# Self-attention with fp16 high and low parts: the low-part score matmul contracts 64 rows, for two row tiles side by side in the upper and lower half of the array

## The chip, the cores and the metric

One core of one Trainium2 chip. The metric is the device time of one execution, in microseconds (us); runs of the kernel before took 2059.68 to 2060.11 us, with a median of 2059.92 us.

## What is computed

The input `x` has four images of 256 channels by 64 x 64 points (4096 points each), in f32. Per image:

```python
xf   = group_norm(x, 32 groups)              # 256 x 4096
f, g = Wq @ xf, Wk @ xf                      # 64 x 4096 each
h    = Wv @ xf                               # 256 x 4096
scores = f.T @ g                             # 4096 x 4096, contraction over 64
beta = softmax(scores, axis=rows)            # over n, for each column m
out  = x + gamma * (h @ beta) + xf
```

## The kernel before

**Precision.** Every f32 operand of a matmul is split into an fp16 high part and an fp16 low part (the rest). A product is then a sum of fp16 matmuls that accumulate in one PSUM bank. For the scores the contraction has only 64 rows, so the 128 rows of the array hold both parts: `F1` has the high part of f in rows 0 to 63 and its low part in rows 64 to 127, `G1` has the high part of g in both halves, `GL` the low part of g in both halves. One matmul `F1.T @ G1` gives high f times high g plus low f times high g, a second one `F1.T @ GL` adds high f times low g and low f times low g.

**Tiling.** The 4096 columns of an image are cut into 16 blocks of 256 (`M`), which makes 64 steps `k` over the four images. The 4096 rows n of the scores are cut into 32 tiles of 128, in 8 groups `g` of 4 tiles. One score group is a PSUM tile `S` of 128 x 1024 f32 (two banks, each with two tiles of 256 columns); `scores(q)` (L299 to L309) issues its 8 matmuls, 2 for each tile (L307, L308). Before it TensorE waits until ScalarE has copied the group before out of `S` (`s_stored`). The copy lands in `SC` (L423); VectorE folds it into the running column maxima (L551 to L558) and later subtracts the maxima (L571); ScalarE takes the exponential twice, once to fp16 (L429, `PH`) and once to f32 (L430); GpSimd makes the low part of the weights (L240, `PL`).

**Order.** The loop over `n` (512 iterations, `n = 8k + g`) is software-pipelined by hand. In iteration n TensorE issues the scores of step k + 2 (`scores(n + 2 * G)`, L382), the transposes that turn the maxima and the outputs (L330, L340, L348), at times a part of the next image's projections, and then `weigh(n)` (L311 to L324), which multiplies the weights of group g with the values: 24 matmuls, 3 for each of 4 tiles and 2 column halves. Steps 62 and 63 have no scores left to issue.

**Projections.** `project_fg(u)` (L275 to L285) makes f and g of 512 points (unit u, 8 per image) with 6 matmuls of 512 columns; the weights `wqkh`, `wqkl` hold Wq in columns 0 to 63 and Wk in 64 to 127, so f comes out in PSUM rows 0 to 63 and g in rows 64 to 127. ScalarE rounds them with three casts (`round_fg`, L432 to L437) and VectorE makes the low parts with three subtractions (`low_fg`, L574 to L579), the last of which raises `fg_done`. For the first image this runs in a prologue (L354 to L361) together with the first 8 score groups; the next 8 score groups run with the value projections (L362 to L371). For the later images the units run inside the loop: `FG_AT` (L48) puts units 0 to 4 in step 13 of an image at g = 3 to 7, and units 5 to 7 in step 14 at g = 3 to 5. The scores of the next image's first block are issued in step 14 and wait for `fg_done` (L381): group g there waits for unit g. `project_v(u)` (L287) makes the values of 4 row tiles with 24 matmuls.

**VectorE's extra work.** In steps 1 to 4 of an image VectorE also measures the next image (L678), in step 5 it makes its variances (L682), in step 6 its inverse roots (L684), in steps 7 to 10 it normalises it (L688).

**Inputs.** SyncE's queue loads the first image, then the weights and gamma (L178 to L183); ScalarE's first cast of the weights waits for all of them (`w_in`, L445).

Of the kernel before, what the change touches and what calls it, by code (L numbers as in the profile page):

```python
# [5 lines left out]
def groupnorm_attention(nc, x, wqT, wkT, wvT, gamma, out):  # L6
    f32, f16, i32 = mybir.dt.float32, mybir.dt.float16, mybir.dt.int32
    ALU, ACT, AX = mybir.AluOpType, mybir.ActivationFunctionType, mybir.AxisListType

    BATCH, C, N = x.shape  # L10
    P = 128
    H = C // P
    CQ = wqT.shape[1]
    M = 256
# [3 lines left out]
    GT = 4  # L18
# [5 lines left out]
    NFG = N // FGW  # L24
# [30 lines left out]
    with ExitStack() as ctx:  # L55
        def sb(name, shape, dt):
            return ctx.enter_context(nc.sbuf_tensor(name, shape, dt))

        def sem(name):
            return ctx.enter_context(nc.semaphore(name))  # L60

        F1 = sb("F1", [P, N], f16)
        G1 = sb("G1", [P, N], f16)
        GL = sb("GL", [P, N], f16)
        V = sb("V", [P, T * VW], f16)
        XH = sb("XH", [P, H, N], f16)
        XL = sb("XL", [P, H, N], f16)

        wqk = sb("wqk", [P, H, P], f32)
        wv = sb("wv", [P, H, C], f32)  # L70
        wqkh = sb("wqkh", [P, H, P], f16)
        wqkl = sb("wqkl", [P, H, P], f16)
        wvh = sb("wvh", [P, H, C], f16)
        wvl = sb("wvl", [P, H, C], f16)
        gam = sb("gam", [P, 1], f32)
# [32 lines left out]
        S = ctx.enter_context(nc.psum_tensor("S", [P, GW], f32))  # L108
# [3 lines left out]
        w_in = sem("w_in")  # L112
# [16 lines left out]
        fg_hi = sem("fg_hi")  # L129
        fg_done = sem("fg_done")  # L130
# [21 lines left out]
        def sc(s):  # L152
# [2 lines left out]
            first = (k % 2) * T * M + g * GW  # L155
            return SC[:, first:first + GW]

        def piece(p):
            return slice(p * PC, (p + 1) * PC)

# [15 lines left out]
        @block.sync  # L176
        def _(sp):
            for q in range(NPC):  # L178
                sp.dma_start(x0[:, :, piece(q)], xv[0, :, :, piece(q)]).then_inc(x0_in[q], 16)
            sp.dma_start(wqk[:, :, 0:CQ], wqT.rearrange("(h p) q -> p h q", p=P)).then_inc(w_in, 16)  # L180
            sp.dma_start(wqk[:, :, CQ:P], wkT.rearrange("(h p) q -> p h q", p=P)).then_inc(w_in, 16)
            sp.dma_start(wv[:, :, :], wvT.rearrange("(h p) v -> p h v", p=P)).then_inc(w_in, 16)
            sp.dma_start(gam[:, :], gamma).then_inc(w_in, 16)  # L183

            def residual_input(k):
                b, j = divmod(k, CPB)
                sp.dma_start(xres[:, :, :], xv[b, :, :, j * M:(j + 1) * M]).then_inc(xres_in, 16)

            def store(k):
                b, j = divmod(k, CPB)  # L190
                sp.wait_ge(out_ready, k + 1)
                sp.dma_start(ov[b, :, :, j * M:(j + 1) * M], RES[:, k % 2, :, :]).then_inc(out_stored[k % 2], 16)

            def load(b, p):
                sp.dma_start(xin[:, :, :], xv[b, :, :, piece(p)]).then_inc(xin_in, 16)

            residual_input(0)
            for k in range(K):
                b, j = divmod(k, CPB)
                if k > 0:  # L200
                    store(k - 1)
                if k + 1 < K:
                    sp.wait_ge(res_ready, k + 1)
                    residual_input(k + 1)
                if b + 1 < BATCH:
                    p = j - STAT_FIRST + 1
                    if 0 <= p < NPC:
                        if p > 0:
                            sp.wait_ge(xin_read, b * NPC + p)
                        elif b > 0:  # L210
                            sp.wait_ge(xl_ready[1], NPC * (b + 1))
                            sp.wait_ge(xl_ready[0], NPC * (b + 1))
                        load(b + 1, p)
                    p = j - NORM_FIRST + 1
                    if j == STAT_FIRST + NPC - 1:
                        sp.wait_ge(xin_read, (b + 1) * NPC)
                        load(b + 1, 0)
                    elif 0 < p < NPC:
                        sp.wait_ge(xl_ready[1], NPC * (b + 1) + p)
                        load(b + 1, p)  # L220
            store(K - 1)
            for parity in range(2):
                sp.wait_ge(out_stored[parity], 16 * K // 2)
# [48 lines left out]
        def _(pe):  # L272
            mm = nc.tensor.matmul

            def project_fg(u, o):  # L275

                b, i = divmod(u, NFG)
                for h in range(H):
                    pe.wait_ge(xl_ready[h], b * NPC + i // 2 + 1)
                n = slice(i * FGW, (i + 1) * FGW)  # L280
                for h in range(H):
                    mm(o, wqkh[:, h, :], XH[:, h, n], start=h == 0, stop=False)  # L282
                    mm(o, wqkl[:, h, :], XH[:, h, n], start=False, stop=False)  # L283
                    m = mm(o, wqkh[:, h, :], XL[:, h, n], start=False, stop=h == H - 1)  # L284
                m.then_inc(fg_ready, 1)  # L285

            def project_v(u, pair):  # L287
                g = u % G
                for i in range(GT):
                    t = g * GT + i  # L290
                    o = O[:, pair, i // 2, (i % 2) * C:(i % 2 + 1) * C]
                    for h in range(H):
                        xh, xl = XH[:, h, t * P:(t + 1) * P], XL[:, h, t * P:(t + 1) * P]
                        mm(o, xh, wvh[:, h, :], start=h == 0, stop=False)  # L294
                        mm(o, xh, wvl[:, h, :], start=False, stop=False)  # L295
                        m = mm(o, xl, wvh[:, h, :], start=False, stop=h == H - 1)  # L296
                m.then_inc(v_ready, 1)

            def scores(q):  # L299

                k, g = divmod(q, G)
                cols = slice((k % CPB) * M, (k % CPB + 1) * M)
                if q > 0:
                    pe.wait_ge(s_stored, q)
                for i in range(GT):
                    f = F1[:, (g * GT + i) * P:(g * GT + i + 1) * P]
                    mm(S[:, i * M:(i + 1) * M], f, G1[:, cols], start=True, stop=False)  # L307
                    m = mm(S[:, i * M:(i + 1) * M], f, GL[:, cols], start=False, stop=True)  # L308
                m.then_inc(s_ready, 1)  # L309

            def weigh(n):  # L311
# [42 lines left out]
            for i in range(NFG + 3):  # L354
                if i < NFG:
                    if i >= 4:
                        pe.wait_ge(fg_done, i - 3)
                    project_fg(i, O[:, i // 2 % 2, i % 2, :])
                if i >= 3:
                    pe.wait_ge(fg_done, i - 2)  # L360
                    scores(i - 3)  # L361
            for g in range(G):  # L362
                scores(G + g)
# [9 lines left out]
            for n in range(K * G):  # L373
                k, g = divmod(n, G)
# [3 lines left out]
                if k + 2 < K:  # L378
                    nb, i = divmod(k + 2, CPB)
                    if i == 0:  # L380
                        pe.wait_ge(fg_done, nb * NFG + g + 1)  # L381
                    scores(n + 2 * G)  # L382
                if g == 2:
                    if k > 0:
# [5 lines left out]
                u = next_fg(k, g)  # L390
# [5 lines left out]
                u = late_values(k, g)  # L396
# [21 lines left out]
        def _(act):  # L418
# [13 lines left out]
            def round_fg(u, o):  # L432
                n = slice(u % NFG * FGW, (u % NFG + 1) * FGW)
                act.wait_ge(fg_ready, u + 1)
                nc.scalar.copy(F1[0:CQ, n], o[0:CQ, :])
                nc.scalar.copy(G1[CQ:P, n], o[CQ:P, :])
                nc.scalar.copy(G1[0:CQ, n], o[CQ:P, :]).then_inc(fg_hi, 1)  # L437

            def round_v(u, pair):
                first = u % G * GT * VW  # L440
# [1 line left out]
                act.wait_ge(v_ready, u + 1)  # L442
                nc.scalar.copy(vh, O[:, pair, :, :].rearrange("p m (t c) -> p (m t) c", c=C)).then_inc(v_hi, 1)  # L443

            act.wait_ge(w_in, 64)  # L445
            nc.scalar.copy(wqkh[:, :, :], wqk[:, :, :])
            nc.scalar.copy(wvh[:, :, :], wv[:, :, :]).then_inc(w_hi, 1)
            for q in range(NPC):
# [17 lines left out]
            for n in range(K * G):  # L466
                k, g = divmod(n, G)
# [3 lines left out]
                u = next_fg(k, g)  # L471
                if u is not None:
                    round_fg(u, O[:, (k + 1) % 2, u % 2, :])
                u = late_values(k, g)
# [4 lines left out]
                if g == 6 and b + 1 < BATCH and NORM_FIRST <= j < NORM_FIRST + NPC:  # L479
                    p = j - NORM_FIRST  # L480
# [5 lines left out]
        def _(dve):  # L486
            ve = nc.vector
# [86 lines left out]
            def low_fg(u, o):  # L574
                n = slice(u % NFG * FGW, (u % NFG + 1) * FGW)
                dve.wait_ge(fg_hi, u + 1)
                ve.tensor_tensor(F1[CQ:P, n], o[0:CQ, :], F1[0:CQ, n], ALU.subtract)
                ve.tensor_tensor(GL[0:CQ, n], o[CQ:P, :], G1[CQ:P, n], ALU.subtract)
                ve.tensor_tensor(GL[CQ:P, n], o[CQ:P, :], G1[CQ:P, n], ALU.subtract).then_inc(fg_done, 1)  # L579

            def low_v(u, pair):
                first = u % G * GT * VW
# [64 lines left out]
            for n in range(K * G):  # L647
                k, g = divmod(n, G)
                b, j = divmod(k, CPB)
                q = n + 2 * G - 1  # L650
# [15 lines left out]
                u = next_fg(k, g)  # L666
                if u is not None:
                    low_fg(u, O[:, (k + 1) % 2, u % 2, :])
                u = late_values(k, g)
                if u is not None:  # L670
                    low_v(u, (k + 1) % 2)
                if g == 5 and b + 1 < BATCH:
                    if STAT_FIRST <= j < STAT_FIRST + NPC:
                        p = j - STAT_FIRST
# [10 lines left out]
                    if NORM_FIRST <= j < NORM_FIRST + NPC:  # L685
                        p = j - NORM_FIRST
# [30 lines left out]
```

## Time and profile before

| | |
|---|---|
| Median of 3 runs | 2059.92 us (2059.68 to 2060.11) |
| Profiled execution, its own time | 2059.63 us |
| Its span, first to last instruction | 2057.8 us |
| Mean granted TensorE clock | 0.997 |
| TensorE matmul busy | 98% of the span |
| VectorE, ScalarE, GpSimd busy | 79%, 78%, 60% |
| Matmuls recorded | 17984 |

The busy share of an engine is the part of the span in which it had an instruction under way. A matmul's duration in the trace is modelled and overlaps that of the next one; the pace of TensorE is read from start to start.

### The profile page before, as it was taken

What the parts mean: (1) busy time and instruction counts of PE and PEld (TensorE: products, weight loads), DVE (VectorE), ACT (ScalarE), POOL (GpSimd) and SP (SyncE); (2) the same over time, 40 slices, a digit from 0 to 9 for tenths busy, and PEclk for the clock granted to TensorE, in tenths of its full rate; (3) what the DMA queues carried; (4) which work ended last, traced back from release to release, by engine and by line L of the source; (5) the groups of instructions that cost most, each with busy time, mean ns of one, the idle gap of its engine ahead of it and who ended that gap; (6) DMA issues with size and microseconds to landing.
All of it is one profiled execution on the core that took longest, in us unless ns stands there. A gap on an engine that the chain in (4) does not pass through costs nothing.

```text
span 2057.8 us, 42838 instructions
## 1 busy us (share of the span) xinstructions
PE 2006.9 (98%) x17984; PEld 1758.9 (85%) x17984; DVE 1620.9 (79%) x2208; ACT 1612.0 (78%) x1699; POOL 1236.6 (60%) x675
## 2 busy tenths in 40 slices
PE   3899999999999999999999999999999999999999
PEld 1688888888888888888888888888878888888887
DVE  8787898877868889887876878988787677777774
ACT  4587788888867777887877778888787787777875
POOL 2066667775545666876544666677645466666666
PEclk9999999999999999999999999999999999999999
DMA  2011101100001110110000111011000000000000
GB/s 94 1 42 53 62 17 42 58 22 16 17 11 57 62 42 16 63 37 22 17 17 32 48 51 37 23 61 37 22 14 14 16 17 22 22 17 22 16 22 21
DMA packets 43585, 66.05 MB, mean 32 GB/s; under 512 B 3201, under 2 KB 36225, under 8 KB 43393
## 3 DMA queue, kind: packets, MB, share of 16 engines
q1 hardware_dynamic: 43392, 63.32, 9.1%
q8 instruction: 141, 2.31, 0.5%
q14 instruction: 52, 0.42, 0.1%
HBM read 46.53 MB, written 16.78 MB: 31 GB/s over the span
## 4 chain that ended last, share of the span: by engine, by line
PE 95%; DVE 2%; ACT 1%; DMA 1%; issue 1%; SPq 0%; ACTq 0%; DVEq 0%
PE O L322 22%; PE O L323 22%; PE O L321 22%; PE S L307 11%; PE S L308 11%; PE O L348 1%; PE O L294 1%; PE O L330 1%; PE O L296 1%; PE O L295 1%; PE MB L340 1%; DMA SC<-x 1%; PE O L284 1%; PE O L283 1%; PE O L282 1%
## 5 line engine op out<-in xcount | busy, mean ns | idle before, releaser
L240 POOL TENSOR_TENSOR PL<-SC,PH 128x1024 f16<-128x1024 f32 x512 | 1092.6, 2135 | 783.2 <-ACT SC L430 782.9
L322 PE MATMUL O<-V,PH 128*128 128x256 f16 x4096 | 1119.7, 273 | 0.0
L321 PE MATMUL O<-V,PH 128*128 128x257 f16 x4096 | 1115.8, 272 | 2.0 <-DVE GL L579 2.0
L323 PE MATMUL O<-V,PL 128*128 128x257 f16 x4096 | 1113.0, 272 | 0.0
L423 ACT ACTIVATE SC<-S 128x1024 f32<-128x1024 f32 x512 | 524.5, 1024 | 337.4 <-PE S L308 334.8
L558 DVE TENSOR_TENSOR XM<-SC,XM 128x512 f32<-128x512 f32 x896 | 619.9, 692 | 156.9 <-ACT SC L423 136.7
L571 DVE TENSOR_TENSOR SC<-SC,MB 128x1024 f32<-128x1024 f32 x512 | 621.0, 1214 | 57.5 <-PE MB L340 56.8
L429 ACT ACTIVATE PH<-SC 128x1024 f16<-128x1024 f32 x512 | 537.6, 1050 | 9.9 <-PE O L323 9.1
L430 ACT ACTIVATE SC<-SC 128x1024 f32<-128x1024 f32 x512 | 536.5, 1048 | 0.0
L307 PE MATMUL S<-G,F 128*128 128x256 f16 x2048 | 477.8, 274 | 11.7 <-ACT SC L423 6.2
L308 PE MATMUL S<-GL,F 128*128 128x256 f16 x2048 | 477.9, 274 | 0.0
L323 PEld LDWEIGHTS O<-V,PL 128*128 128x128 f16 x4096 | 402.5, 98 | 52.1
L321 PEld LDWEIGHTS O<-V,PH 128*128 128x128 f16 x4096 | 394.1, 96 | 60.2 <-issue 2.8
L322 PEld LDWEIGHTS O<-V,PH 128*128 128x128 f16 x4096 | 396.2, 97 | 56.0
L307 PEld LDWEIGHTS S<-G,F 128*128 128x128 f16 x2048 | 201.0, 98 | 39.0 <-DVE GL L579 8.9
L308 PEld LDWEIGHTS S<-GL,F 128*128 128x128 f16 x2048 | 201.0, 98 | 24.0
L585 DVE TENSOR_TENSOR V<-O,V 128x1024 f16<-128x1024 f32 x32 | 39.2, 1225 | 79.9 <-ACT V L443 79.9
L249 POOL TENSOR_SCALAR RES<-xres,rscale,rbias 128x256 f32<-128x256 f32 x128 | 82.3, 652 | 0.0
L564 DVE TENSOR_REDUCE mxc<-O 128x2 f32<-128x512 f32 x64 | 44.2, 691 | 45.8 <-PE O L330 45.8
L443 ACT CAST V<-O 128x1024 f16<-128x1024 f32 x32 | 32.4, 1013 | 53.0 <-PE O L296 53.0
L294 PE MATMUL O<-wvh,XH 128*128 128x256 f16 x256 | 70.3, 275 | 3.4 <-DVE mxc L564 2.2
L295 PE MATMUL O<-wvl,XH 128*128 128x256 f16 x256 | 70.2, 274 | 0.0
(73 smaller groups left out, 980.3 us busy)
## 6 DMA issues: line engine op xcount, KB each, us to landing
xin<-x SPq DMA_DIRECT2D x24, 1024.0 KB, 5.4
xres<-x SPq DMA_DIRECT2D x64, 256.0 KB, 2.7
out<-RES SPq DMA_DIRECT2D x64, 256.0 KB, 2.1
SC<-x SPq DMA_DIRECT2D x4, 1024.0 KB, 8.3
wv<-wvT SPq DMA_DIRECT2D x1, 256.0 KB, 10.2
wqk<-wqT SPq DMA_DIRECT2D x1, 64.0 KB, 10.4
wqk<-wkT SPq DMA_DIRECT2D x1, 64.0 KB, 10.3
gam<-gamma SPq DMA_DIRECT2D x1, 0.5 KB, 9.7
```

The costliest lines, as they stand in the source:

```text
L240: pool.tensor_tensor(PL[:, s % RING, :], sc(s), PH[:, s % RING, :], ALU.subtract).then_inc(pl_ready, 1)
L294: mm(o, xh, wvh[:, h, :], start=h == 0, stop=False)
L307: mm(S[:, i * M:(i + 1) * M], f, G1[:, cols], start=True, stop=False)
L308: m = mm(S[:, i * M:(i + 1) * M], f, GL[:, cols], start=False, stop=True)
L321: mm(o[:, 0:C + 1], PH[:, n % RING, cols], vh, start=t == 0, stop=False)
L322: mm(o[:, 0:C], PH[:, n % RING, cols], vl, start=False, stop=False)
L323: w = mm(o[:, 0:C + 1], PL[:, n % RING, cols], vh, start=False, stop=t == T - 1)
L423: nc.scalar.activation(sc(q), S[:, :], ACT.Copy).then_inc(s_stored, 1)
L429: nc.scalar.activation(PH[:, s % RING, :], sc(s), ACT.Exp, bias=SHIFT)
L430: nc.scalar.activation(sc(s), sc(s), ACT.Exp, bias=SHIFT).then_inc(exp_done, 1)
L558: ve.tensor_tensor(XM[:, :], part, XM[:, :], ALU.max).then_inc(s_maxed, 1)
L571: ve.tensor_tensor(tile, tile, MB[:, 0:M].unsqueeze(1).to_broadcast([P, GT, M]), ALU.subtract).then_inc(sub_ready, 1)
```

## The change

Three things change. First, `project_fg` of an odd unit uses weights with Wk in the first and Wq in the last 64 columns (a third copy block of Wq is loaded behind Wk), so that f and g of odd units come out with the halves exchanged; `round_fg` and `low_fg` follow (`halves`). `F1` then holds the high part of f in rows 0 to 63 for even units and in rows 64 to 127 for odd ones. Second, a score group takes two row tiles from an even unit (places 0 and 1, first bank of `S`) and two from the next, odd unit (places 2 and 3, second bank); `project_v` places the values in the same order, and the waits on `fg_done` ask for both units of a pair. Third, the second score matmul of a tile contracts only the 64 rows that hold the high part of f: the product of the two low parts is no longer computed. These four matmuls are issued between the first two and the last two full ones, in the order upper, lower, upper, lower half.

```diff
-        wqk = sb("wqk", [P, H, P], f32)
+        wqk = sb("wqk", [P, H, P + CQ], f32)
...
+        def tile(g, i):
+
+            return (g - g % 2 + i // 2) * GT + g % 2 * 2 + i % 2
+
+        def halves(u):
+
+            top, bottom = slice(0, CQ), slice(CQ, P)
+            return (bottom, top) if u % 2 else (top, bottom)
...
+            sp.dma_start(wqk[:, :, P:P + CQ], wqT.rearrange("(h p) q -> p h q", p=P)).then_inc(w_in, 16)
...
+                w = slice(i % 2 * CQ, i % 2 * CQ + P)
                 for h in range(H):
-                    mm(o, wqkh[:, h, :], XH[:, h, n], start=h == 0, stop=False)
...
+                    mm(o, wqkh[:, h, w], XH[:, h, n], start=h == 0, stop=False)
...
-                    t = g * GT + i
+                    t = tile(g, i)
...
-                for i in range(GT):
-                    f = F1[:, (g * GT + i) * P:(g * GT + i + 1) * P]
-                    mm(S[:, i * M:(i + 1) * M], f, G1[:, cols], start=True, stop=False)
-                    m = mm(S[:, i * M:(i + 1) * M], f, GL[:, cols], start=False, stop=True)
+                tiles = [slice(tile(g, i) * P, (tile(g, i) + 1) * P) for i in range(GT)]
+                for i in (0, 2):
+                    mm(S[:, i * M:(i + 1) * M], F1[:, tiles[i]], G1[:, cols], start=True, stop=False)
+                for i in (0, 2, 1, 3):
+                    half = slice(0, CQ) if i < 2 else slice(CQ, P)
+                    mm(S[:, i * M:(i + 1) * M], F1[half, tiles[i]], GL[half, cols], start=i % 2 == 1, stop=i % 2 == 0)
+                for i in (1, 3):
+                    m = mm(S[:, i * M:(i + 1) * M], F1[:, tiles[i]], G1[:, cols], start=False, stop=True)
                 m.then_inc(s_ready, 1)
...
-                    pe.wait_ge(fg_done, i - 2)
+                    pe.wait_ge(fg_done, (i - 3) // 2 * 2 + 2)
...
-                        pe.wait_ge(fg_done, nb * NFG + g + 1)
+                        pe.wait_ge(fg_done, nb * NFG + g // 2 * 2 + 2)
...
-                nc.scalar.copy(F1[0:CQ, n], o[0:CQ, :])
-                nc.scalar.copy(G1[CQ:P, n], o[CQ:P, :])
-                nc.scalar.copy(G1[0:CQ, n], o[CQ:P, :]).then_inc(fg_hi, 1)
+                f, g = halves(u)
+                nc.scalar.copy(F1[f, n], o[f, :])
+                nc.scalar.copy(G1[g, n], o[g, :])
+                nc.scalar.copy(G1[f, n], o[g, :]).then_inc(fg_hi, 1)
...
-            act.wait_ge(w_in, 64)
+            act.wait_ge(w_in, 80)
...
-                ve.tensor_tensor(F1[CQ:P, n], o[0:CQ, :], F1[0:CQ, n], ALU.subtract)
-                ve.tensor_tensor(GL[0:CQ, n], o[CQ:P, :], G1[CQ:P, n], ALU.subtract)
-                ve.tensor_tensor(GL[CQ:P, n], o[CQ:P, :], G1[CQ:P, n], ALU.subtract).then_inc(fg_done, 1)
+                f, g = halves(u)
+                ve.tensor_tensor(F1[g, n], o[f, :], F1[f, n], ALU.subtract)
+                ve.tensor_tensor(GL[f, n], o[g, :], G1[g, n], ALU.subtract)
+                ve.tensor_tensor(GL[g, n], o[g, :], G1[g, n], ALU.subtract).then_inc(fg_done, 1)
```

## Rows read from the trace of the kernel before

**Rows 1.** The page: busy time of each engine, and the chain that ended last.

```profile
PE 2006.9 (98%) x17984; PEld 1758.9 (85%) x17984; DVE 1620.9 (79%) x2208; ACT 1612.0 (78%) x1699; POOL 1236.6 (60%) x675
...
PE 95%; DVE 2%; ACT 1%; DMA 1%; issue 1%; SPq 0%; ACTq 0%; DVEq 0%
```

**Rows 2.** Busy time of the engines by stretch: us, then PE, PEld, DVE, ACT, POOL.

```profile
0.00:70.00 70.00, 30.03 (x148) 16.62 (x149) 58.93 (x103) 33.14 (x45) 13.41 (x11) 0.90 0.19 70
70.00:110.00 40.00, 35.81 (x323) 31.18 (x321) 30.15 (x36) 27.82 (x30) 10.67 (x5) 1.00 0.01 1
110.00:500.00 390.00, 390.00 (x3539) 345.52 (x3537) 321.58 (x442) 318.17 (x332) 260.72 (x140) 1.00 0.12 40
```

**Rows 3.** Groups of score matmuls and weight loads: busy us, mean ns, idle before.

```profile
L308 PE MATMUL S<-GL,F 128*128 128x256 f16 x2048 | 477.9, 274 | 0.0
L307 PE MATMUL S<-G,F 128*128 128x256 f16 x2048 | 477.8, 274 | 11.7 <-ACT SC L423 6.2 <-DVE GL L579 5.4
...
L308 PEld LDWEIGHTS S<-GL,F 128*128 128x128 f16 x2048 | 201.0, 98 | 24.0
```

**Rows 4.** TensorE in order of time, one score group: start us, us, line.

```profile
201.80 0.38 PE L340 MATMUL MB<-ident,mxc 128*128 128x128 f32 x2
...
202.02 0.27 PE L307 MATMUL S<-G,F 128*128 128x256 f16 x1
...
202.78 0.27 PE L308 MATMUL S<-GL,F 128*128 128x256 f16 x1
...
202.89 0.27 PE L321 MATMUL O<-V,PH 128*128 128x257 f16 x1
```

**Rows 5.** In order of time: TensorE after a wait, at the start of step 14.

```profile
515.72 0.69 DVE L579 TENSOR_TENSOR GL<-O,G 64x512 f16<-64x512 f32 x1
515.73 0.27 PE L308 MATMUL S<-GL,F 128*128 128x256 f16 x1
...
516.64 0.10 PEld L321 LDWEIGHTS O<-V,PH 128*128 128x128 f16 x1 [0.93 <-issue]
516.67 0.27 PE L321 MATMUL O<-V,PH 128*128 128x257 f16 x1 [0.68 <-DVE GL L579]
...
516.78 0.27 PE L322 MATMUL O<-V,PH 128*128 128x256 f16 x1
```

**Rows 6.** In order of time: units 5 and 7 of the second image, step 14.

```profile
529.18 0.38 PE L284 MATMUL O<-XL,wqkh 128*128 128x512 f16 x1
529.39 0.27 PE L321 MATMUL O<-V,PH 128*128 128x257 f16 x1
...
532.26 0.27 PE L307 MATMUL S<-G,F 128*128 128x256 f16 x1
...
532.80 0.69 DVE L579 TENSOR_TENSOR GL<-O,G 64x512 f16<-64x512 f32 x1
...
539.24 0.27 PE L321 MATMUL O<-V,PH 128*128 128x257 f16 x1
...
541.88 0.27 PE L307 MATMUL S<-G,F 128*128 128x256 f16 x1
...
542.64 0.69 DVE L579 TENSOR_TENSOR GL<-O,G 64x512 f16<-64x512 f32 x1
```

**Rows 7.** VectorE in order of time: its first subtraction of two units in succession.

```profile
509.50 0.69 DVE L577 TENSOR_TENSOR F<-O,F 64x512 f16<-64x512 f32 x1
...
514.32 0.68 DVE L577 TENSOR_TENSOR F<-O,F 64x512 f16<-64x512 f32 x1
```

**Rows 8.** Busy time by step of 29.24 us, columns as in Rows 2: steps 1, 5, 6.

```profile
137.35:166.59 29.24, 29.24 (x268) 26.00 (x267) 24.02 (x33) 23.32 (x25) 18.17 (x11) 1.00 0.17 55
...
254.31:283.55 29.24, 29.24 (x268) 25.99 (x267) 26.30 (x42) 23.32 (x25) 18.17 (x11) 1.00 0.06 19
283.55:312.79 29.24, 29.24 (x268) 26.00 (x267) 27.00 (x46) 23.44 (x25) 18.20 (x11) 1.00 0.06 19
```

**Rows 9.** ScalarE in order of time, start of the kernel.

```profile
23.52 2.00 ACT L451 CAST XH<-SC 128x1024 f16<-128x1024 f32 x2 [7.63 <-DVE SC L540]
```

More of the change, by code:

```diff
@@ L67, in groupnorm_attention @@
         XL = sb("XL", [P, H, N], f16)
-        wqk = sb("wqk", [P, H, P], f32)
+        wqk = sb("wqk", [P, H, P + CQ], f32)
         wv = sb("wv", [P, H, C], f32)
-        wqkh = sb("wqkh", [P, H, P], f16)
-        wqkl = sb("wqkl", [P, H, P], f16)
+        wqkh = sb("wqkh", [P, H, P + CQ], f16)
+        wqkl = sb("wqkl", [P, H, P + CQ], f16)
         wvh = sb("wvh", [P, H, C], f16)
@@ L280, in project_fg @@
                 n = slice(i * FGW, (i + 1) * FGW)
+                w = slice(i % 2 * CQ, i % 2 * CQ + P)
                 for h in range(H):
-                    mm(o, wqkh[:, h, :], XH[:, h, n], start=h == 0, stop=False)
-                    mm(o, wqkl[:, h, :], XH[:, h, n], start=False, stop=False)
-                    m = mm(o, wqkh[:, h, :], XL[:, h, n], start=False, stop=h == H - 1)
+                    mm(o, wqkh[:, h, w], XH[:, h, n], start=h == 0, stop=False)
+                    mm(o, wqkl[:, h, w], XH[:, h, n], start=False, stop=False)
+                    m = mm(o, wqkh[:, h, w], XL[:, h, n], start=False, stop=h == H - 1)
                 m.then_inc(fg_ready, 1)
```

## The prediction

> **What bounds the kernel now.** I read the busy times and the chain that ended last first [rows 1]. TensorE is busy for 98% of the span and makes 95% of the chain, with the other engines at 79% and below; what the change saves on TensorE counts, until another engine is in the way. By stretch [rows 2] TensorE has no idle time from 110 to 500 us (390.00 of 390.00), and the stretches behind it look alike, but for short waits around the units of the next image. Only the first 70 us belong to others: there TensorE is busy for 30.03 and VectorE for 58.93 us. From start to start, not by modelled durations, TensorE's pace is: 8 score matmuls from 202.02 to 202.89, so 0.87 us or 0.109 each [rows 4]. The weight loads are hidden: 98 ns each [rows 3], begun as the matmul ahead of them starts.
>
> The profiled execution took 2059.63 us, 0.3 under the median of the runs; the sum goes by 2059.6.
>
> **Score matmuls.** Before, a group takes 8 slots of 0.109 us. After it are 4 full matmuls and 4 of 64 rows, in two pairs that use different halves of the array and different banks of `S`. If a pair takes one slot, the group takes 6 slots: 2 x 0.109 = 0.218 us less. A pair can't take less than a slot, since a slot goes by columns: a matmul of 512 columns holds TensorE from 529.18 to 529.39, one of 257 for 0.11 [rows 6]; 64 rows still stream 256 columns. Of the 512 groups the first 8 sit in the prologue, where VectorE sets the pace, and 8 beside the first value projections, where TensorE has gaps (35.81 of 40 us) [rows 2]; I count neither. The other 496 give 496 x 0.218 = **-108.1 us**.
>
> **Stagger within a pair.** The second half starts only when its weights are in. After a wait a load stands 0.03 us before its matmul (516.64 to 516.67) [rows 5]. If the lower half's load goes only when the upper matmul has started, the pairs and the full matmul behind them end 0.03 us late in each group: 496 x 0.03 = 14.9 us. If it is pulled ahead, as a load is now, it is nothing. No row decides; I take half, **+7.4 us**, and keep 0 and 14.9.
>
> **Going over between 128 and 64 rows.** Each group changes its shape twice, into the halves and back: 992 times in 496 groups. No row has a matmul of 64 rows. The lower bound is 0: f32 transposes stand directly between fp16 matmuls, two from 201.80 and the next line at 202.02, 0.11 us each [rows 4], so one change of what the array does costs nothing. A gain is excluded, a shape change does no work. The upper bound is that the next matmul waits until the one before has left altogether and then loads: 0.273 from start to modelled end, less the slot of 0.109, is 0.164 us, with the load 0.194 [rows 3, 5]. That is 0 to 992 x 0.194 = 192 us, which is more than the whole gain. I take **0**, because the transposes are the nearest rows, but it is the weakest step. The Trainium skill speaks against it ("TensorEngine Tiling (Array Packing)", Key Properties): changing the tiling mode, not just the tile, drains TensorE. It gives no time for a drain; no row here shows one, and the rivals below carry it.
>
> **The waits on pairs of units.** In step 14 group 4 of the next image's scores now waits for unit 5 and group 6 for unit 7, each projected just one iteration earlier. Unit 5's last matmul gives way at 529.39; the scores of group 4 start at 532.26; VectorE ends the unit at 532.80 + 0.69 = 533.49 [rows 6], and a waiting matmul starts 0.26 after such an end (515.72 + 0.69 against 516.67 [rows 5]). So TensorE would stand from 532.26 to 533.75, 1.5 us. Unit 7: 542.64 + 0.69 + 0.26 = 543.59 against 541.88 [rows 6], 1.7 us. TensorE is the bound and its queue is in order, so `weigh` behind the wait is late too: 3.2 us x 3 images = **+9.6 us**. The wait of 0.68 us at the start of step 14 [rows 5] grows by the 0.22 us by which TensorE comes earlier: **+0.7 us** for three.
>
> **VectorE as the next limit.** With units 0 to 4 of step 13 an iteration takes 0.87 + 6 x 0.215 + 2.64 = 4.80 us on TensorE, and VectorE shows the same 4.82 from unit to unit, with no idle time [rows 7]. At 4.6 us on TensorE VectorE is the limit: 0.2 x 5 units x 3 = **+3 us**. An ordinary step takes 29.24 us and would take 29.24 - 8 x 0.218 = 27.5. VectorE's busy time is 24.0 in steps 1 to 4, which fits; steps 5 and 6, with variances and roots, have 26.30 and 27.00 [rows 8], nearly full. A lead of four groups covers most; I take 0.7 us an image, **+2 us**, with 0 and 6 as ends.
>
> **Edits at nothing.** The third weight transfer of 64 KB, the wider cast and the wider subtraction: ScalarE stands for 7.63 us after its weight casts [rows 9], waiting for VectorE. Without that cover it is under 1 us. The prologue's waits on pairs fall where VectorE is behind anyway. The casts and subtractions of exchanged halves, and the reordered values, have the same sizes and counts.
>
> **Sum.** 2059.6 - 108.1 + 7.4 + 0 + 9.6 + 0.7 + 3 + 2 = 1974.2, so 1974 us. Own range: 1974 - 7 - 3 - 3 = 1961 to 1974 + 7 + 4 = 1985. The Trainium skill ("TensorE: Matmul & The Clock Gate", Part 3, The mechanism) has the matmuls of different tiles starting about 4 ns apart; by that the stagger would be 2 us in place of 7.4 and the sum an estimated 1969.
>
> **Rivals.** (1) *A short drain.* The shape change costs something between the exposed load, 0.03, and just under break-even. Gain without it is 2059.6 - 1974 = 86 us, so break-even is at 86 / 992 = 0.086 us per change. At 0.03 it is 1974 + 30 = 2004, at 0.06 2033, at 0.09 2063. For it: 64 rows are another configuration, unlike a transpose over the full array. Against it: gapless rows [rows 4].
>
> (2) *A full drain, slower than before.* Each change waits for the matmul ahead to end and then loads: 0.164 to 0.194 us. The time is 1974 + 992 x 0.164 = 2137 to 1974 + 192 = 2166, less some 5 us that VectorE then no longer costs: 2132 to 2161. It decides from 0.086 us up. For it: if the array has to be empty, the modelled end is the only end that the rows know. Against: nothing in the trace waits so now. By the rule of the Trainium skill named above ("TensorEngine Tiling (Array Packing)", Key Properties) this rival or the one before it holds.
>
> (3) *The halves don't run together.* Each of the 64-row matmuls takes its own slot; then 8 slots stay, the waits on units stay, and it is 2059.6 + 9.6 = 2069, or a few us more. For it: each matmul here starts a full slot behind the one ahead, never sooner [rows 4]. Against: all those use the same rows of the array.
>
> **How the numbers follow.** Forecast 0.42, short drain 0.23, full drain 0.27, no overlap 0.08. The likeliest is 1974 us, its own range 1961 to 1985. The cases of both signs hold much, so the whole range is wide: from 1960 to 2134, with the full drain beyond its lower edge left out (about 0.17) and some 0.02 below. A difference of 0.2%, 4 us, is about what a measurement of this kernel can tell from none. Faster: 0.42 and most of the short drain, 0.62; within 0.2%: 0.03; slower: 0.27 + 0.08, 0.35.
>
> **What the profile after would show.** Right: in a score group the two starts of a pair of 64-row matmuls stand under 0.04 us apart, the first full matmul behind the halves starts 0.11 after the last pair, and the group takes about 0.67 us from its first matmul to the first of `weigh`. A short or full drain: gaps of 0.03 to 0.19 ahead of the first half and of the full matmul behind. No overlap: four starts 0.11 apart. The waits: TensorE idle some 1.5 us twice in step 14, released by the last subtraction of `low_fg`. VectorE: its idle time in step 6 gone, TensorE waiting there only if I am wrong about the lead. Steps of 27.5 us in place of 29.24 confirm the sum; steps over 29.24 refute it.

## The result, and the profile after

The changed kernel takes 2070.8 us (2068.5 to 2071.3, 5 runs) where the kernel before took 2059.9 beside it: a ratio of 1.0049, with a 95% interval of 1.0034 to 1.0063. It is slower by 11 us. The forecast was 1974 us; the number lies within the wide range, but the sign is the other one. The runs of either kernel fall in two bunches some 2 us apart, the slower one with a slightly lower mean clock (0.994 against 0.995 in the changed kernel), and bunch against bunch the loss is 9 to 10 us.

| | before | after |
|---|---|---|
| Median | 2059.92 us | 2070.81 us |
| Span of the profiled execution | 2057.8 us | 2069.4 us |
| One score group, first start to `weigh` | 0.87 us | 0.86 us |
| One ordinary step | 29.24 us | 29.19 us |
| First reduction of turned maxima in the loop (step 0) | 109.9 us | 116.2 us |

From the page of the changed kernel, the busy times and the groups of the score matmuls and of their loads (busy us, mean ns, idle before); they answer to [rows 1, 3]:

```profile
PE 2007.0 (97%) x17984; PEld 1574.7 (76%) x17984; DVE 1618.8 (78%) x2208; ACT 1613.4 (78%) x1699; POOL 1236.7 (60%) x675
...
L318 PE MATMUL S<-G,F 128*128 128x256 f16 x1024 | 196.6, 274 | 23.0 <-DVE GL L596 16.3
L321 PE MATMUL S<-GL,F 64*128 64x256 f16 x2048 | 201.6, 275 | 0.0
L323 PE MATMUL S<-G,F 128*128 128x256 f16 x1024 | 201.6, 279 | 0.0
L321 PEld LDWEIGHTS S<-GL,F 64*128 64x128 f16 x2048 | 58.3, 94 | 108.7 <-issue 108.7
L323 PEld LDWEIGHTS S<-G,F 128*128 128x128 f16 x1024 | 58.1, 97 | 108.8 <-issue 108.8
```

TensorE is as busy as before, 2007 us against 2006.9, although 2048 matmuls now run in pairs. (Busy time goes by modelled ends, 0.27 us from a start; a gap shorter than that tail doesn't show as idle.) The new thing stands at the weight loads: ahead of each stretch of halves (L321) and of each first full matmul behind it (L323) the loads sit idle for 0.21 us, 512 times each, "issue" by the profile, so no semaphore is what they wait for. Before, all of them began with the matmul ahead. The changed kernel in order of time, one score group, against [rows 4]:

```profile
204.28 0.27 PE L338 MATMUL O<-V,PL 128*128 128x257 f16 x1
204.28 0.21 PEld L318 LDWEIGHTS S<-G,F 128*128 128x128 f16 x2
204.39 0.38 PE L318 MATMUL S<-G,F 128*128 128x256 f16 x2
204.70 0.11 PEld L321 LDWEIGHTS S<-GL,F 64*128 64x128 f16 x4 [0.21 <-issue]
204.70 0.39 PE L321 MATMUL S<-GL,F 64*128 64x256 f16 x4
...
205.02 0.11 PEld L323 LDWEIGHTS S<-G,F 128*128 128x128 f16 x2 [0.21 <-issue]
205.03 0.39 PE L323 MATMUL S<-G,F 128*128 128x256 f16 x2
205.15 0.10 PEld L336 LDWEIGHTS O<-V,PH 128*128 128x128 f16 x1
205.25 0.27 PE L336 MATMUL O<-V,PH 128*128 128x257 f16 x1
```

A row of several matmuls runs from the first start to the last modelled end, so the last start is the end less 0.27 or 0.28. The four halves need 0.39 - 0.28 = 0.11 from first to last start: two pairs, one slot apart. The second full matmul starts at 204.50, its slot ends at 204.61, and the halves start at 204.70: 0.09 lost. The second pair starts at 204.81, its slot ends at 204.92, the full matmul starts at 205.03: 0.11 lost. Six slots of 0.109 and 0.206 us of gaps are 0.86 us, one hundredth less than eight slots. The gain is there, and two changes of shape eat it. (Starts are read to 0.01 us here; the whole step gives the price more sharply, see below.)

The steps say the same. The reduction of the maxima comes once a step; first the changed kernel, then the one before:

```profile
116.15 0.68 DVE L580 TENSOR_REDUCE mxc<-O 128x2 f32<-128x512 f32 x1
143.56 0.69 DVE L580 TENSOR_REDUCE mxc<-O 128x2 f32<-128x512 f32 x1 [0.90 <-PE O L345]
172.75 0.69 DVE L580 TENSOR_REDUCE mxc<-O 128x2 f32<-128x512 f32 x1 [0.91 <-PE O L345]
```

```profile
109.88 0.69 DVE L564 TENSOR_REDUCE mxc<-O 128x2 f32<-128x512 f32 x1
137.35 0.69 DVE L564 TENSOR_REDUCE mxc<-O 128x2 f32<-128x512 f32 x1 [0.91 <-PE O L330]
166.59 0.69 DVE L564 TENSOR_REDUCE mxc<-O 128x2 f32<-128x512 f32 x1 [0.91 <-PE O L330]
```

172.75 - 143.56 = 29.19 against 29.24: 0.05 us a step, 3 us in all. Two slots less in each of 8 groups should have taken 8 x 0.218 = 1.74 us off a step; 16 changes of shape took back 1.69 of it, 0.106 us each. And the changed kernel enters the loop 6.3 us late. The rest is the new waits, here TensorE in step 14 of the first image:

```profile
539.10 0.39 PE L318 MATMUL S<-G,F 128*128 128x256 f16 x2 [1.11 <-DVE GL L596]
...
550.21 0.39 PE L318 MATMUL S<-G,F 128*128 128x256 f16 x2 [1.33 <-DVE GL L596]
```

The idle time counts from the modelled end of the matmul ahead. Its slot had ended 0.16 us earlier, so the two waits cost 1.27 and 1.49, or 2.8 us an image and 8.3 in three; the second and third images show the same 1.11 and 1.33. The balance: +6.3 + 8.3 - 3 = 11.6, which is 2069.4 - 2057.8.

### The profile page after: what moved, and what is told of

It is laid out like the page before. It is cut to its first block, busy times and chain, and to the rows that moved or that the text cites. A ratio compares the mean times of both kernels' runs of the same rounds, so it can differ in the third digit from the quotient of the medians.

```text
span 2069.4 us, 42839 instructions
## 1 busy us (share of the span) xinstructions
PE 2007.0 (97%) x17984; PEld 1574.7 (76%) x17984; DVE 1618.8 (78%) x2208; ACT 1613.4 (78%) x1699; POOL 1236.7 (60%) x675
## 4 chain that ended last, share of the span: by engine, by line
PE 94%; DVE 3%; ACT 1%; issue 1%; DMA 1%; SPq 0%; ACTq 0%; DVEq 0%
PE O L337 21%; PE O L338 21%; PE O L336 21%; PE S L323 8%; PE S L321 8%; PE S L318 5%; PE O L305 1%; PE O L307 1%; PE O L306 1%; PE O L363 1%; PE O L345 1%; PE MB L355 1%; DMA SC<-x 1%; PE O L293 1%; PE O L294 1%
## 5 line engine op out<-in xcount | busy, mean ns | idle before, releaser
L318 PE MATMUL S<-G,F 128*128 128x256 f16 x1024 | 196.6, 274 | 23.0 <-DVE GL L596 16.3
L321 PE MATMUL S<-GL,F 64*128 64x256 f16 x2048 | 201.6, 275 | 0.0
L323 PE MATMUL S<-G,F 128*128 128x256 f16 x1024 | 201.6, 279 | 0.0
L321 PEld LDWEIGHTS S<-GL,F 64*128 64x128 f16 x2048 | 58.3, 94 | 108.7 <-issue 108.7
L323 PEld LDWEIGHTS S<-G,F 128*128 128x128 f16 x1024 | 58.1, 97 | 108.8 <-issue 108.8
L318 PEld LDWEIGHTS S<-G,F 128*128 128x128 f16 x1024 | 99.1, 98 | 39.8 <-DVE GL L596 20.7
```

The costliest lines, as they stand in the source:

```text
L318: mm(S[:, i * M:(i + 1) * M], F1[:, tiles[i]], G1[:, cols], start=True, stop=False)
L321: mm(S[:, i * M:(i + 1) * M], F1[half, tiles[i]], GL[half, cols], start=i % 2 == 1, stop=i % 2 == 0)
L323: m = mm(S[:, i * M:(i + 1) * M], F1[:, tiles[i]], G1[:, cols], start=False, stop=True)
```

## The experiments

**1. Two theories of the loss of 11 us.** First the changed kernel with full height in all score matmuls, then the kernel before with nothing but the waits on pairs.

```diff
-                    half = slice(0, CQ) if i < 2 else slice(CQ, P)
-                    mm(S[:, i * M:(i + 1) * M], F1[half, tiles[i]], GL[half, cols], start=i % 2 == 1, stop=i % 2 == 0)
+                    mm(S[:, i * M:(i + 1) * M], F1[:, tiles[i]], GL[:, cols], start=i % 2 == 1, stop=i % 2 == 0)
```

> The changed kernel with 128 rows in the four low-part matmuls again, everything else as changed. Theory (each change between 128 and 64 rows costs 0.103 us, 992 to 1024 times): 8 slots and no shape change, group 0.87 us, no gaps in it, steps 29.24 us; 2070.8 + 3 = 2074 us if the waits and the start-up keep their whole price, and not less than 2066. Rival (the 64-row pairs cost two slots each, no change of shape costs anything): the same 0.87 us, so this run alone does not part them, but both say that the loss of 11 us is the waits and the start-up. Rival (exchanged halves or the tile order cost time of their own on other engines): casts or subtractions longer than 0.58 and 0.69 us.

Measured: 2073.0 us (2072.3 to 2073.8). The gaps are gone, four low matmuls from 204.36 stand in slots of 0.109:

```profile
204.14 0.38 PE L318 MATMUL S<-G,F 128*128 128x256 f16 x2
204.36 0.60 PE L320 MATMUL S<-GL,F 128*128 128x256 f16 x4
204.80 0.38 PE L322 MATMUL S<-G,F 128*128 128x256 f16 x2
205.01 0.27 PE L335 MATMUL O<-V,PH 128*128 128x257 f16 x1
```

```diff
-                    pe.wait_ge(fg_done, i - 2)
+                    pe.wait_ge(fg_done, (i - 3) // 2 * 2 + 2)
...
-                        pe.wait_ge(fg_done, nb * NFG + g + 1)
+                        pe.wait_ge(fg_done, nb * NFG + g // 2 * 2 + 2)
```

> The kernel before with the two waits on pairs of units alone, nothing else changed. Theory (the whole loss is these waits): inside the loop 1.1 + 1.3 us for each of three images, 7.3 us, and what the later first score group costs in the start-up, up to 6 us: 2067 to 2074 us. Rival (the start-up loss belongs to the wider weights or to the 64-row matmuls): 2067 us and the first turn of the maxima in step 0 within 1 us of 109.9.

Measured: 2072.6 us (2072.0 to 2073.4), a ratio of 1.0060 (1.0046 to 1.0074). Two lines of waits make the whole loss, and more than it. The same two waits stand in step 14 (1.13 and 1.35 us), and the loop is entered 3.9 us later than in the kernel before:

```profile
113.79 0.68 DVE L564 TENSOR_REDUCE mxc<-O 128x2 f32<-128x512 f32 x1
```

The rival that puts the whole loss in the start-up down to the weights or the halves falls: 3.9 of the 6.3 us come without either. What the 64-row matmuls bring for themselves is the changed kernel against full height: 2073.0 - 2070.8 = 2.2 us. By that a change of shape costs (0.218 - 2.2 / 496) / 2 = 0.107 us.

**2. Is the gap a change of shape, and what does it hang on?** Two halves first, then four full ones, then two halves, in the same number of matmuls:

```diff
-                for i in (0, 2):
-                    mm(S[:, i * M:(i + 1) * M], F1[:, tiles[i]], G1[:, cols], start=True, stop=False)
-                for i in (0, 2, 1, 3):
-                    half = slice(0, CQ) if i < 2 else slice(CQ, P)
-                    mm(S[:, i * M:(i + 1) * M], F1[half, tiles[i]], GL[half, cols], start=i % 2 == 1, stop=i % 2 == 0)
-                for i in (1, 3):
-                    m = mm(S[:, i * M:(i + 1) * M], F1[:, tiles[i]], G1[:, cols], start=False, stop=True)
+                for i in (0, 2):
+                    half = slice(0, CQ) if i < 2 else slice(CQ, P)
+                    mm(S[:, i * M:(i + 1) * M], F1[half, tiles[i]], GL[half, cols], start=True, stop=False)
+                for i in (0, 2):
+                    mm(S[:, i * M:(i + 1) * M], F1[:, tiles[i]], G1[:, cols], start=False, stop=True)
+                for i in (1, 3):
+                    mm(S[:, i * M:(i + 1) * M], F1[:, tiles[i]], G1[:, cols], start=True, stop=False)
+                for i in (1, 3):
+                    half = slice(0, CQ) if i < 2 else slice(CQ, P)
+                    m = mm(S[:, i * M:(i + 1) * M], F1[half, tiles[i]], GL[half, cols], start=False, stop=True)
```

> The same matmuls in another order: two halves, four full ones, two halves, so four changes of shape in a group in place of two. The first halves follow weigh and the last are followed by weigh, which writes other banks. Theory (a change of shape costs 0.103 us wherever it stands): 2 x 0.103 more in each of 512 groups, of which some 496 count, 2070.8 + 102 = 2173 us, group 1.07 us to the first of weigh. Rival (the gap is a wait of a matmul for the one ahead that writes the same bank): no gap ahead of the first halves and behind the last ones, only the two inside, 2071 us. Rival (the gap is the first load alone, 0.03): +30, 2101 us.

Measured: 2176.2 us, 105.3 more than the changed kernel for 992 more changes: 0.106 each. In order of time, one group of it:

```profile
208.26 0.27 PE L341 MATMUL O<-V,PL 128*128 128x257 f16 x1
208.47 0.28 PE L319 MATMUL S<-GL,F 64*128 64x256 f16 x2
208.68 0.39 PE L321 MATMUL S<-G,F 128*128 128x256 f16 x2
208.91 0.38 PE L323 MATMUL S<-G,F 128*128 128x256 f16 x2
209.23 0.28 PE L326 MATMUL S<-GL,F 64*128 64x256 f16 x2
209.44 0.28 PE L339 MATMUL O<-V,PH 128*128 128x257 f16 x1
```

Every change is 0.21 from start to start where 0.109 is the slot: 208.26 to 208.47 in, 208.47 to 208.68 out, 209.02 to 209.23 in, 209.23 to 209.44 out. The first and the last join matmuls that write different banks (`O` and `S`), so the rival of the bank falls, and at 0.106 so does the one that put the gap at 0.03. A pair itself takes 0.28, as one matmul: its two halves start within 0.01 us of each other.

**3. Do the halves run together because they lie in different rows?** All four in the upper half, in the place of the choice by `i`:

```diff
-                    half = slice(0, CQ) if i < 2 else slice(CQ, P)
+                    half = slice(0, CQ)
```

> All four 64-row matmuls use the upper half of the array; for the two tiles of the odd unit they so multiply the low part of f instead of the high part. Theory (halves run together only when they lie in different rows, a pair takes one slot): four slots in place of two, 496 x 0.218 = 108 us more, 2179 us; starts 0.11 us apart. Rival (64-row matmuls are simply quick, wherever they lie): no more than 2071 us.

Measured: 2177.9 us, 107 more. The four now need 0.61 - 0.28 = 0.33 from first to last start, three slots:

```profile
206.40 0.38 PE L318 MATMUL S<-G,F 128*128 128x256 f16 x2
206.72 0.61 PE L321 MATMUL S<-GL,F 64*128 64x256 f16 x4
207.26 0.39 PE L323 MATMUL S<-G,F 128*128 128x256 f16 x2
```

**4. The price of a pair, without more changes.** Each pair issued twice:

```diff
-                for i in (0, 2, 1, 3):
+                for i, r in ((0, 0), (2, 0), (0, 1), (2, 1), (1, 0), (3, 0), (1, 1), (3, 1)):
...
-                    mm(S[:, i * M:(i + 1) * M], F1[half, tiles[i]], GL[half, cols], start=i % 2 == 1, stop=i % 2 == 0)
+                    mm(S[:, i * M:(i + 1) * M], F1[half, tiles[i]], GL[half, cols],
+                       start=i % 2 == 1 and r == 0, stop=i % 2 == 0 and r == 1)
```

> Each pair of 64-row matmuls is issued twice, so the low product is added twice; two more pairs in the same stretch, no more changes of shape. Theory (a pair costs one slot of 0.109, a change 0.103, apart from each other): 496 x 0.218 = 108 us more, 2179 us. Rival (the gap belongs to each pair): 496 x 0.42 = 208 us more, 2279 us. Rival (a stretch has a minimum time that two pairs do not fill): less than 60 us more.

Measured: 2178.8 us, 108.0 more, so a pair is 0.109 us, one slot, and the gaps are apart from it.

**5. What the forecast took the change to be:** six slots and no change of shape. From the full-height kernel, the low product of the last two tiles left out:

```diff
-                    mm(S[:, i * M:(i + 1) * M], F1[:, tiles[i]], G1[:, cols], start=True, stop=False)
-                for i in (0, 2, 1, 3):
-                    mm(S[:, i * M:(i + 1) * M], F1[:, tiles[i]], GL[:, cols], start=i % 2 == 1, stop=i % 2 == 0)
+                    mm(S[:, i * M:(i + 1) * M], F1[:, tiles[i]], G1[:, cols], start=True, stop=i == 2)
+                for i in (0, 1):
+                    mm(S[:, i * M:(i + 1) * M], F1[:, tiles[i]], GL[:, cols], start=i == 1, stop=i == 0)
                 for i in (1, 3):
-                    m = mm(S[:, i * M:(i + 1) * M], F1[:, tiles[i]], G1[:, cols], start=False, stop=True)
+                    m = mm(S[:, i * M:(i + 1) * M], F1[:, tiles[i]], G1[:, cols], start=i == 3, stop=True)
```

> The run with 128 rows in all score matmuls, and the low product left out for the last two tiles of each group: six slots in a group and no change of shape, which is what the forecast took the change to be. Theory (the shape changes are what ate the gain, the other terms stand): 2073.0 - 108.1 = 1964.9, plus the 5 us that were put down to VectorE in steps 5, 6 and 13: 1965 to 1970 us. Rival (another engine stands right behind TensorE, so that the time could not have fallen by much anyway): over 2000 us, with waits of TensorE on ScalarE, VectorE or GpSimd in every step.

Measured: 1970.7 us (1969.0 to 1971.5), a ratio of 0.9564 (0.9548 to 0.9580). Its step is 27.5 us (136.63 to 164.13 from reduction to reduction), as forecast. What the next limit costs shows in steps 6 and 7 of each image, behind VectorE's extra work; TensorE waits there for ScalarE's copy of the scores and for VectorE's subtraction of the maxima:

```profile
297.46 0.28 PE L318 MATMUL S<-G,F 128*128 128x256 f16 x1 [0.73 <-ACT SC L437]
...
309.20 0.29 PE L354 MATMUL MB<-ident,mxc 128*128 128x128 f32 x1 [0.79 <-DVE SC L586]
```

From the ends of the slots these are 0.16 us more each, 1.8 us an image. From the first reduction in the loop (115.74 and 111.34) to the last (2029.03 and 1924.23) this kernel is 100.4 us shorter than the one with full height, where 62 steps of 1.74 would be 108.1: the loop loses 7.7 us, 5.5 of them in these two waits, and the other 4.4 us of the difference between the two profiled executions come from the start-up.

**6. Half as many changes, the same slots.** On the kernel of experiment 8: even groups issue each pair twice, odd groups leave the low product out.

```diff
+                low = [(0, 0), (2, 0), (0, 1), (2, 1), (1, 0), (3, 0), (1, 1), (3, 1)] if g % 2 == 0 else []
...
-                    mm(S[:, i * M:(i + 1) * M], F1[:, tiles[i]], G1[:, cols], start=True, stop=False)
-                for i in (0, 2, 1, 3):
+                    mm(S[:, i * M:(i + 1) * M], F1[:, tiles[i]], G1[:, cols], start=True, stop=not low)
+                for i, r in low:
...
-                    mm(S[:, i * M:(i + 1) * M], F1[half, tiles[i]], GL[half, cols], start=i % 2 == 1, stop=i % 2 == 0)
+                    mm(S[:, i * M:(i + 1) * M], F1[half, tiles[i]], GL[half, cols],
+                       start=i % 2 == 1 and r == 0, stop=i % 2 == 0 and r == 1)
...
-                    m = mm(S[:, i * M:(i + 1) * M], F1[:, tiles[i]], G1[:, cols], start=False, stop=True)
+                    m = mm(S[:, i * M:(i + 1) * M], F1[:, tiles[i]], G1[:, cols], start=not low, stop=True)
```

> The kernel with the units moved forward; even groups issue each of their pairs twice, odd groups leave the low product out (their second tile pair too, so the low product is doubled in one half of the rows and missing in the other). Slots and matmuls are the same, the changes of shape are half as many. Theory (only the number of changes counts): 496 x 0.103 = 51 us less than 2060.3, 2009 us. Rival (a longer stretch costs more on the way out, or the even and odd groups cannot be averaged since other engines wait): over 2030 us.

Measured: 2015.9 us, 44.4 less than experiment 8 and 7 more than expected. An ordinary step shrinks from 29.19 to 28.35 us (139.42 to 167.77): 0.84 for 8 changes, 0.105 each, and 62 such steps would be 52 us. What is missing is 2.6 us an image in steps 5 to 10, where VectorE has its extra work. The profile shows two waits of TensorE there, 0.52 and 0.80 us, which are 0.68 and 0.96 from the ends of the slots. The rest is four starts of a score group 0.36 behind the start ahead, 0.25 late each, of which this is one:

```profile
359.03 0.27 PE L341 MATMUL O<-V,PL 128*128 128x257 f16 x1
...
359.39 0.28 PE L320 MATMUL S<-G,F 128*128 128x256 f16 x1
```

0.68 + 0.96 + 4 x 0.25 = 2.6 us, 7.9 in three images, and 52 less 7.9 is the 44 that the loop gained (1902 to 1858 us from its first reduction of the maxima to its last). So the other engines do wait, as the rival had it, but for a small part of its price, and the number of changes counts.

**7. The start-up, first try.** TensorE projects one unit further before it waits for the pair:

```diff
-                if i < NFG:
-                    if i >= 4:
-                        pe.wait_ge(fg_done, i - 3)
-                    project_fg(i, O[:, i // 2 % 2, i % 2, :])
+                for u in (3, 4) if i == 3 else (i + 1,) if i > 3 else (i,):
+                    if u < NFG:
+                        if u >= 4:
+                            pe.wait_ge(fg_done, u - 3)
+                        project_fg(u, O[:, u // 2 % 2, u % 2, :])
```

> The changed kernel; in the start-up TensorE projects unit i + 1 before it waits for the pair and issues the scores of group i - 3. Theory (the start-up loses its 6 us because TensorE stands for 6.75 us before the first scores, with unit 4 behind them): 2070.8 - 3 to 6 = 2065 to 2068 us. Rival (the start-up is paced by VectorE and what is lost is a later rise of the granted clock): within 1 us of 2070.8.

Measured: 2068.5 us (2067.9 to 2070.8), 2.3 less than the changed kernel, and the two spreads overlap. The first reduction in the loop stood at 115.79, hardly earlier. So the first wait was not what decides; neither expectation is met cleanly.

**8. The waits in step 14.** On experiment 7, the later images' units moved forward:

```diff
-    FG_AT = {(FG_FIRST, 3 + i): i for i in range(5)} | {(FG_FIRST + 1, 3 + i): 5 + i for i in range(3)}
+    FG_AT = {(FG_FIRST, 3): (0, 1), (FG_FIRST, 4): (2,), (FG_FIRST, 5): (3,), (FG_FIRST, 6): (4,),
+             (FG_FIRST, 7): (5,), (FG_FIRST + 1, 3): (6,), (FG_FIRST + 1, 4): (7,)}
...
-                    if k % CPB in (FG_FIRST + 1, FG_FIRST + 2):
-                        pe.wait_ge(fg_done, min(b + 1, BATCH - 1) * NFG + (5 if k % CPB == FG_FIRST + 1 else 8))
+                        pe.wait_ge(fg_done, min(b + 1, BATCH - 1) * NFG + (6 if k % CPB == FG_FIRST + 1 else 8))
```

> The kernel of the run before and, for the later images, the units moved forward: two in the third iteration of step 13, then one in each, so that units 6 and 7 stand in the iterations 3 and 4 of step 14. Theory (the waits of 1.1 and 1.3 us in step 14 go, the one of 0.68 at its start grows to 1 or 2): 3 x 1.5 = 4 us less than the run before, 2061 to 2064 us. If all were saved the kernel would stand at the 0.05 us a step that shape changes leave, 2057 us, level with the kernel before. Rival (VectorE, full in step 13, falls behind and hands the wait on): no gain over the run before.

Measured: 2060.3 us (2059.4 to 2062.4), 8.2 less than experiment 7, twice what I had expected. Both waits are gone (8.3 us), and the one at the start of step 14 did not grow: 2.1 us in three images, where the kernel before has 2.0.

```profile
PE O L337 <- DVE GL L596: 2.1, 3, 0.8
```

This is all that TensorE waits for the low parts behind the start-up. The ratio to the kernel before is 1.0003 (0.9994 to 1.0012).

**9. The start-up, second try.** In order of time, what TensorE waits for in the start-up; before, and changed:

```profile
58.20 0.37 PE L307 MATMUL S<-G,F 128*128 128x256 f16 x1 [1.21 <-ACT SC L423]
61.27 0.37 PE L307 MATMUL S<-G,F 128*128 128x256 f16 x1 [1.21 <-DVE GL L579]
64.25 0.40 PE L307 MATMUL S<-G,F 128*128 128x256 f16 x1 [1.11 <-ACT SC L423]
```

```profile
61.96 0.61 PE L318 MATMUL S<-G,F 128*128 128x256 f16 x2 [2.21 <-DVE GL L596]
64.85 0.59 PE L318 MATMUL S<-G,F 128*128 128x256 f16 x2 [1.21 <-ACT SC L438]
67.63 0.60 PE L318 MATMUL S<-G,F 128*128 128x256 f16 x2 [1.12 <-ACT SC L438]
```

In both, VectorE's last unit releases a group at 61 or 62 us. Before it is group 7 and one more follows; in the changed kernel it is group 6 and two follow, 2.9 us each. To let the last units pass ahead, VectorE now takes the maxima two units later:

```diff
-            for i in range(NFG + 3):
+            for i in range(NFG + 5):
...
-                if i >= 3:
-                    maximum(i - 3, 0)
-                    maximum(i - 3, 1)
+                if i >= 5:
+                    maximum(i - 5, 0)
+                    maximum(i - 5, 1)
```

> The kernel with the units moved forward, and in the start-up VectorE takes the maxima of a group two units later, so that the low parts of units 5 to 7 stand ahead of four subtractions' worth of maxima. Theory (what the start-up lost is that the scores of group 6 wait for unit 7, which VectorE ends at 61.9 us behind the maxima, where before only group 7 waited for it): unit 7 is done by about 59 us, the first turn of the maxima in step 0 moves from 115.6 to 112 or 113, and the time is 3 us less, 2057 us. Rival (VectorE's total work paces the start-up, in whatever order): within 1 us of 2060.3.

Measured: 2058.6 us (2057.9 to 2061.1, 11 runs), 1.7 less than experiment 8, and the first reduction in the loop at 111.83. Unit 7 is done at 60.1 and TensorE no longer waits for it:

```profile
60.56 0.59 PE L319 MATMUL S<-G,F 128*128 128x256 f16 x2 [1.21 <-ACT SC L439]
```

The mechanism is there at about half its size. (The reduction stood at 115.62 in the profile of experiment 8, but there the granted clock is 0.66 from 100 to 105 us and here 1.00, so not all of these 3.8 us are the order.) The ratio to the kernel before is 0.9994 (0.9985 to 1.0003): level, not shown to be faster. No version that computes the whole of this product beats the kernel before.

## Why the prediction was wrong

**Going over between 128 and 64 rows** is the step that failed. I took 0, by the f32 transposes that stand gaplessly between fp16 matmuls. They were the nearest rows, but a transpose over the full array is not a change of shape, so the row answered another question. Measured, it is 0.103 us by the gaps of one group, 0.106 by the length of a step, 0.107 by the comparison with full height, 0.106 by doubling the changes, 0.105 by halving them. That is 992 x 0.105 = 104 us, against the -108.1 of the matmuls. My own break-even of 0.086 and bounds of 0 to 0.194 held it. The Trainium skill ("TensorEngine Tiling (Array Packing)", Key Properties) says that changing the tiling mode drains TensorE; the traces agree that going in and coming out cost time, 0.10 us each. Whether the array has to run empty or the load of the first matmul behind a change is only not begun early isn't parted by these runs: that load starts with its matmul, where nearly all others start with the matmul ahead, and takes 0.10 us too. I named that rule as the one against the change and then gave "no cost" the most weight.

**The rivals.** The short drain had the right mechanism, but I ended it "just under break-even", at 0.09, and began the full drain at 0.164. The value lay in the hole between the two cases. The full drain, as I had priced it, is excluded: the next matmul doesn't wait for the modelled end of 0.273, it starts 0.21 after the start of the one ahead. No overlap is excluded by experiments 2 and 3; that its number, 2069, is the nearest to the measured one is chance.

**Score matmuls, -108.1:** right. Experiment 5 has the saving without the changes: its ordinary step is 29.24 - 27.50 = 1.74 us shorter, 108 in 62 steps.

**Stagger, +7.4:** nothing. The halves start within 0.01 us. Here the 4 ns of the Trainium skill ("TensorE: Matmul & The Clock Gate", Part 3, The mechanism) fit the trace, and my half of 0.03 didn't.

**Waits on pairs, +9.6:** right in place and mechanism, 8.3 measured: 1.27 and 1.49 us an image in place of 1.5 and 1.7. Experiment 8 gives 8.2 back. The +0.7 for the wait at the start of step 14 was nothing: TensorE comes no earlier, and the wait is 0.68 us as before.

**The prologue at nothing:** wrong, 6.3 us. I argued that VectorE is behind anyway. It is, and that is why its last unit decides; I didn't ask which group that unit releases. With the pair waits alone (experiment 1), where the granted clock from 75 us on is 1.00 as before, the first reduction in the loop stands at 113.8, so 3.9 us are the wait and the group behind it. The other 2.4 go with a lower granted clock in the changed kernel (0.90 against 1.00 from 75 to 110 us); why it fell there is not shown. It isn't the 64-row matmuls alone: with full height the clock there is 0.95 and the reduction stands at 115.7.

**VectorE as the next limit, +5:** not reached in this kernel. Where it is, in experiment 5, the place was right and the size too small: 7.7 us in the loop. That the times differ by 2073.0 - 1970.7 = 102.3, against my 108.1 - 5 = 103.1, is luck: the shorter start-up of that run makes up for it.

**Chances.** With the change's whole gain hanging on one unmeasured price whose bounds, 0 to 0.194, lay on both sides of break-even, and a rule against zero, 0.42 for zero was too much.

## What to carry to other kernels

Count the changes between array shapes in an order of matmuls like instructions of their own, here 0.10 us each, about one matmul of 256 columns: a stretch of p pairs saves p x 0.109 - 0.206 us, so two pairs are break-even and only longer stretches pay. In this kernel a stretch over two groups would need four banks for `S`, where `O` holds four, `XM` and `MB` one each; it wasn't tried. And where a wait on one unit becomes a wait on two, look up what the last unit releases, in the start-up too: the two changed wait lines alone cost 12.5 us here.

## What was not expected of the hardware

The gap hardly follows TensorE's clock. At the lower level (granted 0.50, so 1.2 GHz) a group of the changed kernel looks so, first the stretch (columns as in [rows 2]), then TensorE in order of time:

```profile
43.40:44.80 1.40, 1.40 (x8) 0.51 (x9) 1.37 (x3) 0.53 (x1) 0.00 (x0) 0.50 0.00 0
```

```profile
43.37 0.61 PE L318 MATMUL S<-G,F 128*128 128x256 f16 x2 [6.75 <-DVE GL L596]
43.91 0.61 PE L321 MATMUL S<-GL,F 64*128 64x256 f16 x4
44.45 0.61 PE L323 MATMUL S<-G,F 128*128 128x256 f16 x2
44.85 0.63 PE L293 MATMUL O<-XH,wqkh 128*128 128x512 f16 x1
```

The kernel before at the same level, one group from its first matmul to the one behind it:

```profile
41.03 0.39 PE L307 MATMUL S<-G,F 128*128 128x256 f16 x1 [4.24 <-DVE GL L579]
...
42.71 0.63 PE L282 MATMUL O<-XH,wqkh 128*128 128x512 f16 x1
```

A slot is 0.213 us there. Eight of them take 42.71 - 41.03 = 1.68 us; the changed group takes 44.85 - 43.37 = 1.48, or 0.20 less, where two slots fewer would be 0.43 less. So two changes cost 0.23, about 0.11 each, against 0.106 at 2.4 GHz. A wait for a number of the array's own cycles would have doubled. This is one group in each kernel, read to 0.01 us.
